# Both ends of a head-attention stage reordered: first scores, last scatters and the next stage's first loads

## The reference

```python
x = x + _L0_xattn_ref(_layernorm(x), ctx, ...)      # attention over a latent width of 128
x = x + _L0_ffn_ref(_layernorm(x), ...)             # gated feed-forward, 512 -> 2048 -> 512, fp8 products
x = x + _L1_xattn_ref(_layernorm(x), ctx, ctx, gamma)
x = x + _L1_ffn_ref(_layernorm(x), ...)             # 8 experts, 2 per row

def _L1_xattn_ref(q, k, v, gamma):                  # 8 heads of width 32
    qk = einsum('bhdq,bhdl->bhql', qh, kh) / sqrt(32)
    return gamma * einsum('bhql,bhdl->bhdq', softmax(qk), vh)

def _L1_ffn_ref(x, gate_w, gate_b, bias, w1, b1, w2, b2):
    scores = xf @ gate_w.T + gate_b + bias
    top_scores, top_idx = top_k(scores, 2); gates = softmax(top_scores)
    h = silu(einsum('td,ehd->teh', xf, w1) + b1)    # hidden width 352
    y = einsum('teh,edh->ted', h, w2) + b2
    return sum over the two chosen experts of gate * y
```

## Time and profile before

| what | us |
|---|---|
| median of 3 runs (lowest, highest) | 888.57 (888.16, 890.78) |
| the profiled execution's own time | 893.75 |
| its span | 892.0 |
| PE busy | 750.1 (84% of the span) |
| VectorE busy | 582.3 (65%) |
| ACT busy | 399.3 (45%) |
| POOL busy | 351.3 (39%) |

### The profile page before, as it was taken

One profiled execution on the slowest core, in us unless ns is written; L12 is line 12 of the kernel. 1 busy time (PEld: TensorE's weight loads), 2 busy tenths in 40 slices (PEclk: granted clock), 3 DMA queues, 4 the chain that ended last, 5 costly groups with the idle time before them and its releaser, 6 DMA issues. The chain is left out here.

```text
span 892.0 us, 14252 instructions
## 1 busy us (share of the span) xinstructions
PE 750.1 (84%) x4263; PEld 310.0 (35%) x4263; DVE 582.3 (65%) x1086; ACT 399.3 (45%) x741; POOL 351.3 (39%) x352
## 2 busy tenths in 40 slices
PE   3888989559999999859999999999951299999993
PEld 1433443224444444202122222222221155555551
DVE  4668786538585859556888888997646045555552
ACT  1533344126363636137677767767841122222220
POOL 2455554200202021233556568567366023333333
PEclk9999999759999999969899999999985689999998
DMA  7999530050828187223334445443313548889964
GB/s 260 287 126 273 180 122 0 1 174 4 292 70 299 66 313 259 63 72 91 77 96 107 106 122 150 103 131 121 84 61 152 131 84 130 123 128 126 132 95 60
DMA packets 114150, 117.51 MB, mean 132 GB/s; under 512 B 54808, under 2 KB 78232, under 8 KB 113824
## 3 DMA queue, kind: packets, MB, share of 16 engines
q1 hardware_dynamic: 102976, 94.48, 37.2%
q0 software_dynamic: 10384, 22.02, 14.6%
q10 hardware_dynamic: 720, 0.13, 0.1%
HBM read 43.61 MB, written 59.56 MB: 116 GB/s over the span
## 5 line engine op out<-in xcount | busy, mean ns | idle before, releaser
L1193 ACT ACTIVATE l_pt<-l_b 128x512 f32<-128x512 f32 x256 | 139.3, 595 | 54.3 <-PE l_b L1089 42.8
L1704 POOL DMA_INDIRECT out<-ex_y,ex_tag x39 | 61.5, 1576 | 133.1 <-DMA out<-ex_y,ex_tag 56.1
L1600 PE MATMUL ex_hp<-w1h,ex_xt 128*128 x312 | 78.5, 321 | 19.0 <-DMA ex_xt<-slots_x 18.1
L1264 DVE TENSOR_REDUCE l_negm<-l_a 128x2 f32<-128x1024 f32 x64 | 75.3, 1221 | 26.2 <-PE l_a L1034 26.2
L1620 PE MATMUL ex_yp<-w2h,ex_ht 128*128 (+1 forms) x234 | 76.9, 383 | 4.9 <-DVE ex_ht L1664 3.5
L1639 ACT ACTIVATE ex_hf<-ex_pre 128x352 f32<-128x352 f32 x39 | 19.4, 496 | 121.1 <-DVE ex_pre L1659 121.1
L1264 DVE TENSOR_REDUCE h_negm<-l_a 128x2 f32<-128x1024 f32 x56 | 66.0, 1221 | 11.7 <-PE l_a L1034 11.5
L598 PE MATMUL f_gp<-f_xt,wg 128*128 128x512 fp8e4 x256 | 67.4, 387 | 3.8 <-ACT f_y L648 2.7
L1100 PE MATMUL l_pv<-l_pt,l_vt 128*32 128x512 f32 x512 | 69.9, 619 | 0.0
L1108 PE MATMUL l_sm<-l_pt,ones_f 128*32 128x512 f32 x512 | 69.7, 617 | 0.0
L598 PE MATMUL f_up_ps<-f_xt,wg 128*128 128x512 fp8e4 x256 | 67.0, 385 | 0.0
(11 more groups left out here) (245 smaller groups left out, 1486.5 us busy)
## 6 DMA issues: line engine op xcount, KB each, us to landing
slots_x<-empty SPq DMA_DIRECT2D x8, 2376.0 KB, 11.0
slots_x<-empty SPq DMA_DIRECT2D x7, 2112.0 KB, 13.4
h_stack<-h_parts SPq DMA_DIRECT2D x96, 64.0 KB
l_stack<-l_parts SPq DMA_DIRECT2D x96, 64.0 KB
f_stage<-in_w SPq DMA_DIRECT2D x8, 704.0 KB, 4.2
l_ctx<-in_ctx SPq DMA_DIRECT2D x8, 512.0 KB, 7.6
f_stage<-in_w SPq DMA_DIRECT2D x8, 512.0 KB
h_kf<-in_ctx SPq DMA_DIRECT2D x16, 256.0 KB, 3.1
```

The lines of the kernel that those rows point to most:

```text
L1193: act.activation(weights_at(u, c, h)[:, :], B[t % 2][:, :], ACT.Exp, scale=SCALE).then_inc(b_ok, 1)
L1264: dve.tensor_reduce(negm[u % 2][:, 2 * half:2 * half + 2, j], A[half][:, :, :], AX.X, ALU.max, negate=True)\
L1600: mm = pe.matmul(HP[i % 2][:, 0:H], xt[i % AHEAD][:, xp * FC + f, :], w1p[wp][:, bass.ds(e, 1), f * H:(f + 1) * H], start=k == 0, stop=k = ...
L1704: pool.indirect_dma_start(out=out, out_offset=bass.IndirectOffsetOnAxis(ap=tags[i % TAGS][:, 0:1].bitcast(U32), axis=0), in_=y[i % YS][:, ...
```

## The change

Six edits. (1) The rows of ones are set by POOL instead of VectorE, for unit 0 in the feed-forward stage before `power(0)`, for unit 1 after `F.power(pool, neg_half, 2)`. (2) PE begins head attention with the first scores; the quads of unit 1 are made in the first four cycles of unit 0, one in each, instead of two before the loop and two in it; VectorE makes the statistics of unit 2 ahead of the maxima of unit 1. (3) ACT waits for the negated gamma in `result`, not before its first exponential. (4) The batches become 4, 4, 3, 3, 1, 1 tiles; batch 2 is chosen at the end of unit 13, placed in unit 14 and sent (six scatters) in unit 15, and the orders at the end are rewritten. (5) The bias and the tiles 0 and 1 with their tags are loaded by SP within head attention, the bias once the last row sums are made, the tiles once the row table is there and the scatters have landed. For this the `PT` ring and the bias share one room, the tiles lie in the first stack, and the buffers outlive the stage. (6) `R.row` signals `table_ok` instead of being waited for on VectorE.

```diff
-                    if not more and m == 8:
-                        dve.memset(F.stack[F.M0:F.M0 + 1, 0, :, :], 1.0).then_inc(F.set_ok, 1)
...
+                    pool.wait_ge(res_ok, g * G)
+                    pool.memset(F.stack[F.M0:F.M0 + 1, 0, :, :], 1.0).then_inc(F.set_ok, 1)
+                    pool.wait_ge(F.set_ok, 1)
                     F.power(pool, neg_half, 0)
...
+class FirstTiles:
+    AHEAD = 4
+    TAGS = 8
+    def __init__(self, nc, st, F, R, D, H, E):
+        self.room = st.enter_context(nc.sbuf_tensor("t_room", [P, 8 * D], F32))
+        self.b1s = self.room[:, 0:E * H].rearrange("p (e h) -> p e h", e=E)
+        tiles = F.stack[:, :, :, :].rearrange("p a h d -> p (a h d)").rearrange("p (k c t) -> p k c t", k=self.AHEAD, t=P)
...
-    BATCHES = [range(0, 4), range(4, 8), range(8, 12), range(12, 15), range(15, 16)]
+    BATCHES = [range(0, 4), range(4, 8), range(8, 11), range(11, 14), range(14, 15), range(15, 16)]
...
+            sp.wait_ge(sum_ps, TC * NU)
+            sp.dma_start(T.b1s, b1.to_broadcast([P, E * (b1.shape[1] // E)])).then_inc(T.b1_in, 16)
             for j in range(NU - 3, NU):
                 store_rows(j)
+            sp.wait_ge(table_ok, 1)
+            for j in range(NU - KEPT, NU):
+                sp.wait_ge(sent[j % KEPT], 32 * (j // KEPT + 1))
+            rows = [T.row_of(sp, slots_x, i) for i in range(2)]
+            for i in range(2):
+                T.load_tile(sp, slots_x, rows[i], i)
+            for i in range(2):
+                T.load_tag(sp, slots_x, rows[i], i)
...
-            for j in range(EARLY):
-                a_quad(1, j)
...
-                    if i % 2:
+                    if u == 0 and i < TC:
+                        a_quad(1, i)
+                    elif i % 2:
...
             mix(NU)
             turn_rows(NU - 2)
+            last_rank(3)
             mix(NU + 1)
-            last_rank(3)
             turn_rows(NU - 1)
+            last_rank(4)
             mix(NU + 2)
-            last_rank(4)
+            last_rank(5)
...
             def result(u):
                 act.wait_ge(pv_ps, TC * u + TC)
+                act.wait_ge(ng_ok, 1)
...
-            act.wait_ge(ng_ok, 1)
...
+            F.statistics(dve, X, 2)
             for j in range(EARLY):
                 maxima(1, j)
-            F.statistics(dve, X, 2)
-            dve.memset(stack[1][M0:M0 + 1, 0, :, :], 1.0).then_inc(set_ok, 1)
...
             row_statistics(NU - 2)
             normal_rows(NU - 2)
+            choose(3)
             normalise(NU - 1)
-            choose(3)
+            gates(3)
+            place_batch(3)
             row_statistics(NU - 1)
             normal_rows(NU - 1)
-            gates(3)
-            place_batch(3)
             choose(4)
             gates(4)
             place_batch(4)
+            choose(5)
+            gates(5)
+            place_batch(5)
             tile_table()
...
             F.power(pool, neg_half, 2)
+            pool.wait_ge(F.rstd_ok, 3)
+            pool.memset(stack[1][M0:M0 + 1, 0, :, :], 1.0).then_inc(set_ok, 1)
+            pool.wait_ge(set_ok, 2)
...
-                for n in range(2):
+                for n in range(3):
                     first = BATCHES[n][-1] + 5
-                    if first <= u < first + 2:
+                    if n < 2 and first <= u < first + 2:
                         send(n, BATCHES[n][2 * (u - first):2 * (u - first) + 2])
+                    if n == 2 and u == first:
+                        send(n, BATCHES[n])
...
             add(NU - 2)
-            send(2, BATCHES[2][0:2])
             row_power(NU - 2)
             with_reciprocals(NU - 1)
             low_rows(NU - 2)
             add(NU - 1)
             row_power(NU - 1)
-            send(2, BATCHES[2][2:4])
+            send(3, BATCHES[3])
             low_rows(NU - 1)
-            send(3, BATCHES[3])
             send(4, BATCHES[4])
+            send(5, BATCHES[5])
...
-            load(0)
-            load(1)
-            sp.dma_start(b1s[:, :, :], b1.to_broadcast([P, E * H])).then_inc(b1_in, 16)
             for i in range(2, TILES):
-                load(i)
```

More of the change, by code:

```diff
@@ L925, in head_attention @@
         mrow = [F.mrow, sb("mrow1", [HU * TC, P], BF16)]
-        PT = [[sb(f"pt{r}{h}", [P, D]) for h in range(HU)] for r in range(RING)]
+        PT = [[T.room[:, (HU * r + h) * D:(HU * r + h + 1) * D] for h in range(HU)] for r in range(RING)]
         pvs = [sb(f"pvs{k}", [P, D]) for k in range(2)]
@@ L947, in head_attention @@
         base, end = sb("base", [P, E]), sb("end", [P, E])
[L948 removed]
+        passed, skipped = (PT[1][2 + k][:, 0:TILES * E].rearrange("p (t e) -> p t e", e=E) for k in range(2))
         expert_f, skip_f, row_f = sb("expert_f", [P, TILES]), sb("skip_f", [P, TILES]), sb("row_f", [P, TILES])
@@ L970, in head_attention @@
         hi_ok, lo_ok, both_ok, slots_ok, step_ok = (sem(n) for n in ("hi", "lo", "both", "slots", "step"))
-        over_ok, weight_ok, tag_ok, gates_ok = sem("over"), sem("weight"), sem("tag"), sem("gates")
+        over_ok, weight_ok, tag_ok, gates_ok, table_ok = sem("over"), sem("weight"), sem("tag"), sem("gates"), sem("table")
         sent = [sem(f"sent{k}") for k in range(KEPT)]
@@ L1545, in experts @@
         w1p, w2p = EW.w1, EW.w2
-        b1s = sb("b1s", [P, E, H])
-        xt = [sb(f"xt{k}", [P, 2 * FC, P], BF16) for k in range(AHEAD)]
+        b1s, xt, tags = T.b1s, T.xt, T.tags
         pre = [sb(f"pre{k}", [P, H]) for k in range(2)]
@@ L1552, in experts @@
         ht = [sb(f"ht{k}", [P, 2, HC, P], BF16) for k in range(2)]
-        tags = [sb(f"tag{k}", [P, R.tag]) for k in range(TAGS)]
         y = [sb(f"y{k}", [P, D]) for k in range(YS)]
@@ L1558, in experts @@
         YP = [ps(f"yp{k}", [P, D]) for k in range(2)]
-        b1_in, edge_ok = sem("b1"), sem("edge")
-        xt_in = [sem(f"xt{k}") for k in range(AHEAD)]
-        tag_in = [sem(f"tag{k}") for k in range(TAGS)]
+        b1_in, edge_ok, xt_in, tag_in = T.b1_in, sem("edge"), T.xt_in, T.tag_in
         added = [sem("added0"), sem("added1")]
@@ L1574, in _ @@
         def _(sp):
-            def load(i):
-                row = sp.value_load(R.row[0:1, i:i + 1], min_val=0, max_val=slots_x.shape[0] - P)
+            for i in range(2, TILES):
+                row = T.row_of(sp, slots_x, i)
                 wait(sp, h_ps, i - AHEAD + 1)
-                sp.dma_start_transpose(xt[i % AHEAD][:, :, :], slots_x[bass.ds(row, P), 0:D].bitcast(BF16)).then_inc(xt_in[i % AHEAD], 16)
+                T.load_tile(sp, slots_x, row, i)
                 if i >= TAGS:
                     landed(sp, i - TAGS)
-                sp.dma_start(tags[i % TAGS][:, :], slots_x[bass.ds(row, P), R.tag_at:R.tag_at + R.tag]).then_inc(tag_in[i % TAGS], 16)
-            load(0)
-            load(1)
-            sp.dma_start(b1s[:, :, :], b1.to_broadcast([P, E * H])).then_inc(b1_in, 16)
-            for i in range(2, TILES):
-                load(i)
+                T.load_tag(sp, slots_x, row, i)
         @block.tensor
```

42 lines of the change are left out of this document (29 added, 13 removed).

## The result

The changed kernel takes **861.22 us** (median of 4 runs, 857.03 to 864.30) against 888.37 for the kernel before in the same comparison: a ratio of 0.9686, 95% interval 0.9641 to 0.9731. Forecast were 864.0 and a range of 859.5 to 872.5. The profiled execution took 864.30 (span 862.6), 29.4 us of span less than the one of before.

What follows compares the result with a forecast made beforehand. PE was busy 84% of the span, with most of the rest lost at the stages' seams; terms -2.5, -6.7, -7.9 and -7.5 sum to -24.6, so 888.6 becomes 864.0 us, range 859.5 to 872.5.

Steps and rivals of the forecast that it cites:

- Feed-forward, -2.5: Last feed-forward group: without VectorE's memset PE's wait shrinks to 0.5 (1.4 saved), slow products give 1.1; between -1.3 and -3.0.
- the bound of 2.1: POOL's memset of 2048 elements takes at most 2.1 us; expected to cost nothing, or 2.1 if its cover were missing.
- First scores, -6.7: Start of head attention: first exponential at about 382.4, cycle 4 at about 392.5 instead of 399.21; bounds -4.5 and -8.0.
- rival A: PE's slow clock level lingers at the seams: first scores -4.5, all together -19.2, giving 869.4; chance 22%.
- Batches, +1.2: Batch 2 in units 13 to 15 delays unit 15's fourth quad: +1.2, between 0 and +4.
- the tail, -7.9: End of head attention: ten scatters instead of twelve, starting earlier, end at 682.5; -7.9 with the batches' 1.2 inside, -5.0 to -9.5.
- Rival B: Batch 2 in units 13 to 15 costs 5.4 like batches 0 and 1, not 1.2: -20.4, 868.2; chance 12%.
- Hand-over, -7.5: Start of the experts: early bias and tiles bring y of tile 0 to 18.8 after the last scatter's landing; -4.5 to -9.
- the landing T: Landing of the last scatter, put at about 694.6 in the kernel before: stage start 695.3 less 0.7 for the seam.
- Rival D: Experts' stage ends later than 6 us after the landing, or scatters land later: hand-over -3, tail -5, 871.4; chance 9%.
- The sum, -24.6: Whole kernel: -2.5 feed-forward, -6.7 first scores, -7.9 tail with batches, -7.5 hand-over, taken from 888.6.

Runs made afterwards that it cites:

- the reciprocals first: Changed kernel with one more edit: in unit 1 POOL multiplies unit 0's reciprocals ahead of the keys of unit 4; 855.85 us, ratio 0.9611.

## Why the prediction was right

The cause and the sum hold; two terms were right for reasons that were partly wrong.

**Feed-forward, -2.5: measured -2.6**, in three comparisons of profiles. The wait shrank by 1.0 and not by 1.4 (0.92 is left, not 0.5), and the slow products went altogether, 1.45 where the prediction took 1.1. POOL's memset cost nothing; that of unit 1 took 1.80 us, inside the bound of 2.1.

**First scores, -6.7: measured -7.0.** The timeline worked out was near: the first exponential at 381.37, against 382.4 less the 2.5 saved before it and plus the 1.8 by which this execution came later to G, 381.7. Predicted was one term for all edits here. The runs divide it: the wait 4.9, what VectorE no longer has between the quads 1.1, PE's order 1.0. The low level ended before 391.9, so rival A's -4.5 did not come. (The price in that bound was somewhat high: eight products took 1.94 at the low level and 1.06 at the full one, 0.88 more and not 1.1.)

**Batches, +1.2 with the tail, -7.9 together: measured -8.5** (+0.45 from R3 to R15, with other slow spots in it, and -8.97). The rows agree with the steps: ten scatters, most of them 1.27 us apart, 14.65 from `row_power(15)` to S where 14.9 was predicted, and `choose(3)` ahead of the refinement. Batch 2 in the middle cost 0.3 to 0.5 in most executions, not 1.2, and 1.9 in two. That the term came out above the forecast was partly luck: in five of ten profiles with the new batches the pause of about 1 us in the last unit was there too, and they give 7.1 or 5.5. Rival B's 5.4 for batch 2 was not seen. Nor is 5.4 what a batch costs by reductions alone: 3.8 of it are the first two units (17.12 and 18.06 against twice 15.69), and the 1.6 of the third (17.32) came at the full clock, with an idle of 0.97 us on PE for which the profile names no releaser and which six of the fourteen profiles don't have. The rule of the Trainium skill on the two sides of the SBUF ("SBUF — State Buffer", section "SBUF: two separate sides"), by which each scatter would wait for a cast of VectorE, would have made the term -6.2. The row speaks against it here: 658.85 to the next at 660.13, beside VectorE's small operations for batch 4, is 1.28, where the scatters behind it are 1.27 apart.

**Hand-over, -7.5: measured -8.7, of which 7.1 is the edit.** The size is right, two steps are not. The first is the landing T: the prediction put it 4.2 after S by taking 0.7 for the seam of before. It is 1.9 after S in the changed kernel, and if before is no different, that seam was 3.2. Counted from T, the changed kernel did nearly what was predicted: stage start at T + 5.9 (predicted 6.1), first product at T + 7.2 (7.2), first bias add at T + 11.0 (10.1), Y at T + 20.0 (18.8). But in the kernel before, the first product then stood at T + 7.4 and not at T + 5.1, and Y at T + 28.6 and not at T + 26.3. With T in its place the same steps would have given -9.8; the changed kernel's Y came 1.2 later than they say, which leaves -8.7. That the two errors partly cancel is luck. The second is what gave the gain: the prediction counted the early tiles as a part of the edit that costs 2 us and frees the bias add. They cost nothing and give 0.3; the bias gives nearly all, and two tiles and two tags issued ahead of the stage's end use up what they save. Rival D's condition, a stage that ends later than T + 6, did not come (T + 5.9); SP's issues do hold the stage's end, as the forecast itself had it.

**Not foreseen: -2.9 between R2 and R3.** No edit touches that stretch, and the whole change isn't needed for it: in the kernel before with only the row of ones moved it was 17.30, and in two changed kernels with a part undone the low level came as well (18.12 and 18.57). After pauses of 1.4 to 1.65 and 0.74 the clock falls in some executions and not in others, 4 of 12. So as far as the profiles tell, these 2.9 are luck of the two executions compared. The Trainium skill's rule on frequent short idles ("TensorE: Matmul & The Clock Gate", section "A second HAM failure mode: psum-queue depth-cycling"), which I had weighed for unit 0, fits those four profiles, two units further on, and not the other eight. With the reciprocals first the pause was gone, and so was the low level. In unit 0 PE came out of the low level in spite of such waits.

**The sum, -24.6: the medians differ by 27.2.** The four terms read from the marks give -26.8, and -25.2 without the 1.6 that was chance at the hand-over. How the other 2 us divide between the edits and slow stretches that came in fewer executions, the runs don't settle. Nor is 27.2 firm to that degree. If the part that each of the six kernels lacks is taken off its ratio by the marks, they give 0.971 to 0.979 for the changed kernel, a gain of 18 to 26 us (an estimate); the two with only a further edit at the hand-over, in a later comparison, have 0.9678 and 0.9658, in line with the 0.9686. The profiles show one thing that goes with this. In unit 9 PE pauses for about 1 us in the profile of before and in all seven profiles from chips 5 and 3, in some of them in units 13 and 15 too; the changed kernel's profile and the five from chips 10 and 8 have none of these pauses. Whether the chip makes the difference was not tried.

## What to carry to other kernels

A wait in front of a loop should stand where its value is read: 4.9 of 7.0 us at the first scores hung on one line. When the start of a stage is made earlier, follow what sets the end of its first unit, not the first instruction: 4.4 us at the first exponential were 1.0 at the mark. Before loads are put ahead of a stage's end, see whether the issue itself delays that end: beside the bias, one tile ahead was worth 3.0 and two tiles with two tags 0.3.

## What the runs showed of the hardware

- The stage behind indirect scatters starts 5.06 us after the last one's end in six profiles in which POOL waits for their landing and SP is done earlier, though SP could act on the landing after 1.87; with SP alone waiting, 3.44.
- Units repeat to 0.02 us where PE has no pause (units 4 to 6 are 15.69 in all fourteen profiles). The second unit of batches 0 and 1 takes 18.06 or about 19.6 (once 20.99) behind the same two pauses of 1.24 and 0.74: at a granted clock of 1.00 in the first case, 0.91 (once 0.84) in the others. The unit behind batch 0 takes 15.69, or 17.2 to 17.3 at the full clock with about 1 us of idle. Several such spots in one execution make differences of some us between executions.
- In the feed-forward stage the low clock level followed the pause of 1.79 to 1.91 us in three of three profiles, and the pause of 0.84 to 0.97 in none of eleven. After the pauses of 1.4 to 1.65 and 0.74 in unit 2 it came in four profiles of twelve.
- ACT's table load takes 1.28 us in all four places of each profile read. "ScalarE activation tables: per-element evaluation and per-set limits" of the Trainium skill, section "What a function is on this engine", gives 1283 ns for it, and the traces agree.
